# A graph network's layers: TensorE reads two of the three bf16 parts of the features as the upper half words of f32 arrays

## The reference, cut to what matters

```python
def _max_cut_grad(x, src, dst, edge_weight, num_nodes):
    msg = x[src] * edge_weight[:, None]
    return jax.ops.segment_sum(msg, dst, num_segments=num_nodes)

def lift_step(h, wb):                      # 8 times
    W, b = wb
    g = _l2_normalize(_max_cut_grad(h, src, dst, edge_weight, N))
    out = jnp.concatenate([h, g], axis=1) @ W + b
    return (_l2_normalize(out), None)

def proj_step(h, wb):                      # 4 times
    W, b = wb
    g = _max_cut_grad(h, src, dst, edge_weight, N)
    out = jnp.concatenate([h, g], axis=1) @ W + b
    return (jnp.tanh(out), None)
```

## Time and profile before

| | |
|---|---|
| median of 3 runs | 11221.48 us (11203.65 to 11251.74) |
| profiled execution, its own time | 11271.17 us |
| span of its instructions | 11269.5 us |
| mean granted TensorE clock | 0.792 of full speed |
| DVE busy | 9343.8 us (83%) |
| PE matmuls busy | 7516.8 us (67%) |

### The profile page before, as it was taken

How to read it: one execution, slowest core, us unless ns; L and a number is a source line. 1 busy time by engine, 2 the same in 40 slices (tenths; PEclk the granted TensorE clock), 3 DMA queues, 4 the chain that set the end, 5 groups by cost and what they waited for, 6 DMA issues and landing times.

```text
span 11269.5 us, 344658 instructions
## 1 busy us (share of the span) xinstructions
PE 7516.8 (67%) x130038; PEld 5063.0 (45%) x130039; DVE 9343.8 (83%) x19419; ACT 3160.2 (28%) x7975; POOL 5206.8 (46%) x5783
## 2 busy tenths in 40 slices
PE   2555555400877877877877887786777777777773
PEld 2444444300766766766766776674222222222221
DVE  8777777668877877877877877777999999999995
ACT  0111111048222222222222222222444444444441
POOL 3777777610321321221221231133877777777771
PEclk9999999975988988988988988896555555555555
DMA  4111111157644744754754655562222222222221
GB/s 173 25 25 25 26 25 25 30 176 242 206 150 149 212 148 149 210 152 149 212 149 151 198 171 161 167 200 60 37 36 36 36 35 36 36 36 34 36 34 19
DMA packets 719352, 1177.38 MB, mean 104 GB/s; under 512 B 177346, under 2 KB 340241, under 8 KB 715001
## 3 DMA queue, kind: packets, MB, share of 16 engines
q1 hardware_dynamic: 435480, 1024.95, 28.7%
q0 software_dynamic: 146832, 68.64, 5.8%
q10 hardware_dynamic: 136012, 67.95, 2.4%
HBM read 1018.50 MB, written 140.22 MB: 103 GB/s over the span
## 4 chain that ended last, share of the span: by engine, by line
PE 31%; DVE 24%; issue 19%; ACT 3%; POOL 2%; DVEq 1%; DMA 1%; ACTq 0%; POOLq 0%; SPq 0%
PE psum L1964 10%; PE psum L1932 10%; PE psum L1947 6%; DVE space L1444 3%; DVE space L1478 2%; PE psum L2039 2%; DVE space L1440 2%; DVE space L1477 2%; DVE space L1412 2%; PE psum L2009 2%; ACT space L1595 2%; DVE space L1482 2%; DVE space L1489 2%; DVE space L1422 2%; PE psum L2024 1%
## 5 line engine op out<-in xcount | busy, mean ns | idle before, releaser
L792 POOL DMA_INDIRECT space<-feature_table,space x2000 | 2422.6, 1211 | 615.2 <-issue 614.9
L717 POOL TENSOR_TENSOR claim_out<-claim_in 128x1 f32<-128x1 f32 x1199 | 309.7, 258 | 4533.3 <-DMA table<-space 2424.7
L2055 PE MATMUL psum<-w_mix,space 64*128 64x448 f32 x4144 | 1833.8, 982 | 0.0
L1627 ACT ACTIVATE space<-psum 128x375 f32<-128x375 f32 x2400 | 938.8, 435 | 2885.3 <-PE psum L1932 2880.6
L728 POOL DMA_INDIRECT slots<-space x1568 | 1511.6, 964 | 465.4 <-issue 412.1
L1143 DVE TENSOR_TENSOR space<-psum,space 128x320 f32<-128x320 f32 x2400 | 1066.4, 486 | 748.6 <-PE psum L1947 722.7
L1932 PE MATMUL psum<-space 128*32 128x125 fp8e4 x72000 | 1342.5, 223 | 239.5 <-issue 238.2
L1964 PE MATMUL psum<-space 128*128 128x96 bf16 x24000 | 1289.7, 207 | 220.6 <-issue 159.9
L1932 PEld LDWEIGHTS psum<-space 128*32 128x32 bf16 x72000 | 1077.2, 97 | 494.1 <-issue 484.7
L1964 PEld LDWEIGHTS psum<-space 128*128 128x128 fp8e4 x24000 | 1101.1, 97 | 379.4 <-issue 263.3
L1153 DVE TENSOR_TENSOR space<-space 128x320 f32<-128x320 f32 x2400 | 1062.7, 484 | 1.4 <-DVE space L1149 1.1
(11 more groups left out here) (278 smaller groups left out, 11875.5 us busy)
## 6 DMA issues: line engine op xcount, KB each, us to landing
space<-marks SPq DMA_DIRECT2D x2400, 320.0 KB
marks<-space SPq DMA_DIRECT2D x100, 640.0 KB, 3.2
space<-distances ACTq DMA_DIRECT2D x200, 320.0 KB
space<-block_ids SPq DMA_DIRECT2D x198, 200.0 KB
slots<-space SPq DMA_DIRECT2D x82, 448.0 KB, 9.7
space<-feature_table,space POOLq DMA_INDIRECT x2072, 2.7
space<-src_rows SPq DMA_DIRECT2D x102, 320.0 KB, 4.0
slots<-space POOLq DMA_INDIRECT x1608, 2.1
```

The source lines that it names most:

```text
L792: g.indirect_dma_start(out=gathered_rows[0:SLOTS, half, t, :], out_offset=None, in_=feature_table, in_offset=bass.IndirectOffsetOnAxis(ap= ...
L1627: a.activation(to[:, s0:s1, :, :], pair_picked[:, bank, 0:(s1 - s0) * PICK_COLS].rearrange("p (k c r) -> p k c r", k=s1 - s0, r=CAP), ACT.Copy
L2055: last = mm(radial[:, 2 * ring + odd, 0:MIX_S + MIX_V], hidden[odd * HIDDEN:(odd + 1) * HIDDEN, slot, upper * LANES:(upper + 1) * LANES], ...
```

## The change

`split_h` no longer casts packed bf16 copies. The first part is now the upper half word of each word of `h` itself (a truncated bf16, where the cast rounded), the second the upper half word of a new f32 array `h_left` = `h` - first part. The third part is cast as before, by the second subtraction, into a packed bf16 array `h_least`. Of four instructions for a chunk two are left, both subtractions, and in both the second operand is now a bf16 view with a step of 4 bytes. On PE the number and order of matmuls in `gather` is the same; for two of the three parts the stationary operand is read with a step of 4 bytes instead of 2. `h_left` and `h_least` take the same number of words of SBUF as the packed parts took, so nothing behind them moves.

```diff
         h = carve(BLOCKS_PADDED, D)
+        h_words = space[:, carve.at - BLOCKS_PADDED * D:carve.at]
         hg = carve(BLOCKS_PADDED, 2 * D)
         work = carve(BLOCKS_PADDED, D)
         loads_at = carve.at
-        parts_words = carve(BLOCKS_PADDED * PARTS * D // 2)
-        parts = parts_words.bitcast(BF16).rearrange("p (b c d) -> p b c d", c=PARTS, d=D)
+        left_words = carve(BLOCKS_PADDED * D)
+        h_left = left_words.rearrange("p (b d) -> p b d", d=D)
+        h_least = carve(BLOCKS_PADDED * D // 2).bitcast(BF16).rearrange("p (b d) -> p b d", d=D)
+        h_top, left_top = (t.bitcast(BF16).rearrange("p (b d k) -> p b d k", d=D, k=2)[:, :, :, 1]
+                           for t in (h_words, left_words))
+        parts = (h_top, left_top, h_least)
...
             def split_h(c, chain):
                 at = CHUNK_BLOCKS[c]
-                chain(v.tensor_copy(parts[:, at, 0, :], h[:, at, :]))
-                chain(v.tensor_tensor(work[:, at, :], h[:, at, :], parts[:, at, 0, :], ALU.subtract))
-                chain(v.tensor_copy(parts[:, at, 1, :], work[:, at, :]))
-                last = v.tensor_tensor(parts[:, at, 2, :], work[:, at, :], parts[:, at, 1, :], ALU.subtract)
+                chain(v.tensor_tensor(h_left[:, at, :], h[:, at, :], h_top[:, at, :], ALU.subtract))
+                last = v.tensor_tensor(h_least[:, at, :], h_left[:, at, :], left_top[:, at, :], ALU.subtract)
                 if c + 1 == DENSE_CHUNKS:
                     last.then_inc(parts_ready, 1)
...
-                                          parts[:, q * SRC_PER_TILE + s, c, :], cells[:, :, g, CAP * s:CAP * (s + 1)],
+                                          parts[c][:, q * SRC_PER_TILE + s, :], cells[:, :, g, CAP * s:CAP * (s + 1)],
```

More of the change, by code:

```diff
@@ L1314, in _ @@
                 with dve.Fori(first, first + layers, 1) as layer:
-                    token = layer_step.enter(layer - first, DENSE_CHUNKS * (4 + 3) + DENSE_CHUNKS - 1 if lift
-                                             else DENSE_CHUNKS * 3)
+                    token = layer_step.enter(layer - first, DENSE_CHUNKS * (4 + 1) + DENSE_CHUNKS - 1 if lift
+                                             else DENSE_CHUNKS * 1)
                     def weigh(j, q):
```

## The result

The changed kernel takes 11286.8 us (median of 6 runs, 11272.3 to 11319.0), against 11224.8 us (6 runs, 11203.7 to 11251.7) for the kernel before on the same chip. The ratio is 1.0047, with a 95% interval of 1.0034 to 1.006: **slower by 0.47%, some 53 us**, where 35 us less were forecast (the two medians alone lie 62 us apart, which is 0.55% and within that interval).

What follows compares the result with a forecast made beforehand. DVE's queue at layer ends was taken to be on the path, with PE and DVE both nearly full in gather. 47.6 us saved less 12.7 given back made 34.9, from 11221.5 to 11187 us; range 11145 to 11235.

Steps and rivals of the forecast that it cites:

- Its own signs of being wrong: Forecast is wrong if clean gather units change, or DVE newly waits between the bias of output 6 and the last split.
- the swallowed gain: Rival: late instructions or tables set the gather stage's end, so an earlier start only moves pauses; 11221 us, chance 0.10.
- The casts removed: DVE's splits at layer ends: 3.55 us less a layer, twelve layers, plus 5.0 ahead of layer 0; 47.6 us saved.
- The subtractions that stay: DVE's subtractions in the splits, now with a strided second operand: no cost, within 0.01 us each.
- The strided weights: PE's gather weight loads with a step of 4 bytes: zero cost; upper bound 688 us.
- the rival of 11875 us: PE's gather: strided weight loads run at half rate through one shared way into the array, 688 us more; chance 0.13.
- What is given back: PE's earlier gather start meets the `table` store: 6.3 us behind proj and 6.4 behind lift layers, 12.7 us lost.
- The link between the landing of `table` and a stop after 53 loads: In a layer's first gather, PE's instructions come late during the store; loads resume 0.31 us behind its landing.
- the rival of -48 in which nothing is given back: The gather's stop is unrelated to the `table` store, so the full 47.6 us stay: 11174 us, chance 0.25.

Runs made afterwards that it cites:

- e1_after_pad8: Changed kernel with 8 empty DVE instructions ahead of the layers, putting the lift layers' chunk loop back in its old place: 11202.6 us, ratio to before 0.9964.
- e4_before_again: The kernel before, unchanged, run for a second profile: 11257.7 us (1 run).
- after: The changed kernel itself, without empty instructions: 11286.8 us, ratio to before 1.0047.
- e2_strided_with_casts: Changed kernel with both casts put back, into an unused array, PE still reading strided parts: 11248.4 us, ratio to before 1.0002.
- the pad of 64: Changed kernel with 64 empty DVE instructions ahead of the layers: 11150.8 us (1 run); timed again, 11166.0 us, ratio to before 0.9945.

## Why the prediction failed, step by step

**The failed step** is the sum's treatment of DVE's stream: the casts were priced by their own time only, and the text ahead of the prediction said that "all else on DVE keeps its order". Order was kept, but place was not. No term and no rival had the cost of a branch by its place; it stood at nothing without a reason. In its stead stand 24 late branches (+96 us) with a second pause behind each, 110.6 us of idle DVE; 90.7 us of it reach the lift gather stages, and the new pause ahead of output 6 adds 2.9. Its own signs of being wrong stayed silent: the clean units are unchanged, and DVE meets no new wait between the bias of output 6 and the last split. The rivals looked for a loss on PE, in transfers and in the swallowed gain, all near the edit; this one sits in a loop behind the edit that wasn't touched. The prediction gave 0.67 to a result within 0.5%; that the measured 0.47% lies there is luck, since it is a gain of some 40 us and a loss of some 93 that no term had.

**The casts removed: right.** For the ends of lift layers the forecast was 3.55 us. In the changed kernel the pair shown gives 3.21, and in `e1_after_pad8` 3.58; its eight "rests" are 28.6 us less than those of `e4_before_again` (746.4 and 717.8), 3.57 each. From the first split ahead of layer 0 to PE's start it is 13.26 us before and 8.24 after: 5.0, as forecast.

Behind proj layers it is 8.5 us for three (240.7 and 232.2), 2.8 each rather than 3.55, and there the prediction had the path wrong. DVE's part became 3.58 us shorter, but PE then waits for its own queue. PE's branch back of the layer loop, behind the same proj layer before and in the changed kernel, and DVE's last split in the latter:

```profile
L1986 PEldq COMPARE_BRANCH  x1: 3957/3957/3957, 7338.3 to 7338.3; - x1
```

```profile
L1989 PEldq COMPARE_BRANCH  x1: 3637/3637/3637, 7375.9 to 7375.9; - x1
```

```profile
7378.54 0.42 DVE L1210 TENSOR_TENSOR space<-space 128x256 bf16<-128x256 f32 x1
```

Before, the branch ends at 7342.2, and PE starts at 7343.60, 0.15 us behind the last split. In the changed kernel the last split ends at 7378.96 and the branch at 7379.55, and PE starts at 7379.83. In all three such starts of both `after` and `e1_after_pad8` PE starts 0.28 us behind its branch's end and 0.5 to 1.2 us behind the split. The profile still puts PE's idle time down to DVE's split there.

**The subtractions that stay: right.** Groups by line and shape of the changed kernel, beside the earlier trace rows:

```profile
L1209 DVE TENSOR_TENSOR space<-space 128x1024 f32<-128x1024 f32 x39 | 47.6, 1219 | 0.6
L1210 DVE TENSOR_TENSOR space<-space 128x1024 bf16<-128x1024 f32 x39 | 47.8, 1225 | 1.3
```

1219 and 1225 ns with a strided operand, 1226 with packed ones.

**The strided weights: right, and the rival of 11875 us falls.** The group of loads, beside the earlier trace rows:

```profile
L1935 PEld LDWEIGHTS psum<-space 128*32 128x32 bf16 x72000 | 1090.4, 98 | 489.1 <-issue 480.4
```

A clean unit has its 60 loads in 0.86 us as before, and the reading alone is worth 1.0002 in `e2_strided_with_casts`. The rule of the Trainium skill ("SBUF — State Buffer", section on the DMA port swizzle), by which two bf16 elements within 16 bytes are read at no loss, is borne out for weights too.

**What is given back: wrong mechanism.** The link between the landing of `table` and a stop after 53 loads held only on one side. Behind lift layers the landing is now at +2.40 us from PE's start, well behind the 53rd load, and there is no stop: 0 us for the 6.4 forecast. Behind proj layers the stop grew. Changed kernel, beside the earlier trace rows:

```profile
7379.83 0.21 PE L1992 MATMUL psum<-zeros 128*128 128x32 bf16 x1 [5.79 <-DVE space L1210]
7379.96 1.39 PEld L1935 LDWEIGHTS psum<-space 128*32 128x32 bf16 x53
...
7383.68 0.19 POOL L722 TENSOR_TENSOR claim_out<-claim_in 128x1 f32<-128x1 f32 x1 [171.09 <-DMA table<-space]
7383.96 0.14 PEld L1935 LDWEIGHTS psum<-space 128*32 128x32 bf16 x7 [2.61 <-issue]
```

The loads go on at +2.5, +2.8 and +3.0 us from PE's start before and at +3.9, +4.1 and +4.1 now: some 4 us for the 6.3 forecast. They follow the landing by -0.16 to 0.32 us, and in `e1_after_pad8` by 0.25 to 0.64, so no fixed distance. A store under way doesn't make a stop by itself, either: behind the lift layers it lands 2.4 us after PE's start, when the 60 loads are long through, and none of them was late. PE's own branch of the layer loop fits both sides. It takes 3.3 to 4.0 us between any two layers; behind proj layers it ends 4.0 to 5.0 us before the loads go on in all nine cases of the three kernels, like the second pause on DVE, and behind lift layers it has ended 6.0 to 6.6 us before PE's start in the two changed kernels (9.6 to 10.2 before), so that a pause of that length would be over. No run moved this branch alone, so the cause is argued and not shown. The stop is worth no more than 4 us; with the 0.75 us of each later start, some 6 us are given back behind proj layers. That this is near the 6.3 forecast is luck, for the forecast had it from the landing.

**The sum without the place.** With the loop back in its old place the change is worth -40 us (-26 to -55 by the interval of `e1_after_pad8`), between the forecast of -35 and the rival of -48 in which nothing is given back. The interval holds both, so this agreement is no proof of the term that was given back; the casts' own gain is shown by the stages above. The range failed because it held only costs of the instructions that were edited.

## What to carry to other kernels

Taking a handful of instructions away moves every loop behind them in that engine's stream. Here a loop of 274 fell on a place where each branch back costs 3 to 5 us in place of 0.2, with a second pause of 1 to 4 us behind it; so look at "issue" waits and at the records of the branch in loops that were not edited, and count how often they are taken. The test is cheap: a few empty instructions ahead of the loop, here 4, and the same comparison is worth making before a good change is dropped for being slower. A price for each edited instruction, however exact, is only half of a forecast when the program has loops behind it.

## What the hardware showed beyond that

The branch back on DVE: 0.19 to 0.27 us, or 3.1 to 5.2 us, with a period of 128 instructions in the place, and behind a late one a second pause at a fixed place of the stream. The Trainium skill ("Advanced Engine Details and Errata", section "Control Flow Timing") gives about 108 ns for a compare-and-branch. The record alone is 50 to 74 ns in this loop, what follows it starts 0.19 us later at best, and the late ones are far from either.

PE's granted clock in the dense stage isn't the same in each execution. Windows of the last layer's dense stage, before and in the changed kernel:

```profile
7706.00:7735.00 29.00, 28.86 (x147) 28.75 (x148) 7.29 (x10) 12.41 (x31) 0.00 (x0) 0.50 0.00 1
```

```profile
7741.00:7754.00 13.00, 13.00 (x130) 13.00 (x128) 5.72 (x7) 10.12 (x26) 0.00 (x0) 1.00 0.01 1
```

The granted clock is 0.50 (1.2 GHz) in the first and 1.00 (2.4 GHz) in the second. PE is busy all through both, with 147 matmuls in 29 us, 197 ns each, and 130 in 13 us, 100 ns each. In the stretch ahead of these it did much the same in both: in 31 us it was busy for 20.0 at a clock of 0.56 before, and for 19.6 at 0.50 in the changed kernel. In the stage table it is the 12.9 us of the last layer's rest (71.6 against 58.7), and again 12 us of the proj layers' rest in one kernel (220.5 with the pad of 64 against 232.2). What decides it no run here shows. The profiled executions here have none, one or two such fast stages, so two profiles can be 25 us apart for it.
